# A two-layer attention and expert block: setup, routing, the second layer's keys and values and the first expert tile taken into the first attention

## What is computed

```
x = x + tanh(g_xattn[0]) * L0_xattn(ctx, layernorm(x), mask, ...)   # Perceiver attention
x = x + tanh(g_ffn[0])   * L0_ffn(layernorm(x), weights, indices)   # experts, given routing
x = x + tanh(g_xattn[1]) * L1_xattn(layernorm(x), ctx, ...)         # cross attention to ctx
x = x + tanh(g_ffn[1])   * L1_ffn(layernorm(x), gate_w, w1, w2, w3) # experts, top-2 routing
```

## Time and profile before

| | |
|---|---|
| median of 3 runs | 4273.21 us (4272.74 to 4275.18) |
| the profiled execution | 4271.42 us |
| its span in the profile | 4269.7 us |
| TensorE busy (matmul) | 3954.1 us, 93% |
| VectorE, ScalarE, GpSimd busy | 2978.6, 1977.3, 1009.8 us |
| mean granted TensorE clock | 0.965 of full |

### The profile page before, as it was taken

One profiled execution on the slowest core, in us unless ns is written; L12 is line 12 of the kernel. 1 busy time (PEld: TensorE's weight loads), 2 busy tenths in 40 slices (PEclk: granted clock), 3 DMA queues, 4 the chain that ended last, 5 costly groups with the idle time before them and its releaser, 6 DMA issues. The chain is left out here.

```text
span 4269.7 us, 68747 instructions
## 1 busy us (share of the span) xinstructions
PE 3954.1 (93%) x23968; PEld 3192.9 (75%) x23968; DVE 2978.6 (70%) x4625; ACT 1977.3 (46%) x2806; POOL 1009.8 (24%) x1012
## 2 busy tenths in 40 slices
PE   5999999998499999999988999958999999999998
PEld 3566655564399999999974555548999999999998
DVE  3766666765476676676634888657887887778885
ACT  3655555554154444444423544504444444444443
POOL 3221121210011011011013566403222222222221
PEclk9999999999699999999998999969999999999999
DMA  2000000000366666666640122116666666666664
GB/s 94 20 32 30 30 30 19 23 17 20 110 215 205 208 207 206 207 207 206 206 146 18 60 81 78 40 46 213 215 208 211 214 209 214 210 212 211 209 213 124
DMA packets 376608, 578.80 MB, mean 136 GB/s; under 512 B 25960, under 2 KB 186792, under 8 KB 376488
## 3 DMA queue, kind: packets, MB, share of 16 engines
q1 hardware_dynamic: 344024, 503.50, 35.4%
q0 software_dynamic: 26208, 61.68, 5.8%
q10 hardware_dynamic: 6256, 12.06, 0.8%
HBM read 518.31 MB, written 58.86 MB: 135 GB/s over the span
## 5 line engine op out<-in xcount | busy, mean ns | idle before, releaser
L1115 DVE TENSOR_TENSOR e_WL<-e_raw,e_WH 128x2048 fp32r<-128x2048 f32 x418 | 957.3, 2290 | 475.5 <-ACT e_WH L1064 473.0
L1064 ACT ACTIVATE e_WH<-e_raw 128x2048 fp32r<-128x2048 f32 x418 | 798.8, 1911 | 796.5 <-PE bank L1042 581.4
L1026 PE MATMUL bank<-e_xh,e_WH 128*128 128x256 f32 x3968 | 1127.0, 284 | 38.7 <-ACT e_hf L1080 19.1
L1026 PE MATMUL bank<-e_xl,e_WH 128*128 128x256 f32 x3968 | 1126.5, 284 | 0.0
L1026 PE MATMUL bank<-e_xh,e_WL 128*128 128x256 f32 x3968 | 1126.4, 284 | 0.0
L1026 PEld LDWEIGHTS bank<-e_xh,e_WH 128*128 128x128 f32 x3968 | 765.6, 193 | 42.2 <-issue 28.6
L1026 PEld LDWEIGHTS bank<-e_xl,e_WH 128*128 128x128 f32 x3968 | 765.5, 193 | 2.3
L1026 PEld LDWEIGHTS bank<-e_xh,e_WL 128*128 128x128 f32 x3968 | 765.3, 193 | 0.0
L1042 PE MATMUL bank<-e_WH,e_hh 128*128 128x512 f32 x1360 | 534.9, 393 | 0.0
L1042 PE MATMUL bank<-e_WH,e_hl 128*128 128x512 f32 x1360 | 529.6, 389 | 0.0
L1042 PE MATMUL bank<-e_WL,e_hh 128*128 128x512 f32 x1360 | 528.9, 389 | 0.0
(11 more groups left out here) (216 smaller groups left out, 6097.6 us busy)
## 6 DMA issues: line engine op xcount, KB each, us to landing
e_raw<-in_w SPq DMA_DIRECT2D x262, 1024.0 KB, 5.3
e_raw<-in_w SPq DMA_DIRECT2D x312, 512.0 KB, 4.4
y<-e_Yo ACTq DMA_DIRECT2D x23, 512.0 KB, 2.9
a_X<-in_x SPq DMA_DIRECT2D x32, 256.0 KB, 2.6
a_R<-in_x SPq DMA_DIRECT2D x32, 256.0 KB, 3.8
x<-a_R SPq DMA_DIRECT2D x32, 256.0 KB, 2.0
a_X<-x SPq DMA_DIRECT2D x32, 256.0 KB, 3.4
x<-a_X SPq DMA_DIRECT2D x32, 256.0 KB, 2.0
```

What stands on the lines that cost most here:

```text
L1026: mm = nc.tensor.matmul(up[n % RING][:, q * ROWS:q * ROWS + ROWS], w, x[:, c, :], start=(c == 0 and i == 0), stop=(c == DC - 1 and i == 2))
L1064: act.activation(WH[:, p, :], raw[:, s, :], ACT.Copy).then_inc(high_ready.sem, 1)
L1115: dve.tensor_tensor(WL[:, p, :], raw[:, p % 2, :], WH[:, p, :].bitcast(F32), ALU.subtract)\
```

## The change

Setup, routing and the second attention's keys and values are no longer parts of their own. They stand in `attention0`, on each engine's list ahead of body -1 and in its steps. What moves:

- The gate, routing and small parameter loads (14) are issued from ScalarE's queue at its start, ahead of the tanh. SyncE's queue loads `ctxT` and `wk1` first, then x, `wv1` and the weights (one load more, `wlkvT` in two), and the zeros of the spare rows last.
- TensorE does the counting matmuls, then ten groups of keys and values ahead of body -1; six more and the 32 inversion matmuls follow in its steps. ScalarE adds the key bias and stores each group to new DRAM tensors `kT1` and `V1` (a ring of two). The value bias is added in `attention1`, on the transposed output.
- The weight split of `attention0` is in three parts, between the groups of keys and values.
- In body 7 GpSimd gathers tile 0's x, SyncE loads its first pieces, ScalarE and VectorE split three (steps 8, 10, 13), and VectorE norms x (10, 14); in body 8 TensorE transposes it. Two more pieces are loaded behind the last x1 stores.
- SyncE no longer waits for the x1 stores at the block's end; ScalarE does in `experts`. The attention's semaphores are given back after the first experts.
- In `experts`, for both layers, tile 0 is written out. The pieces not yet split and those of tile 1 are split one behind each slot. In layer 1, which has nothing split ahead, three pieces are split before the first slot.
- `attention1` loads `kT1` and `V1`, 2 MB each, behind its weights.

The core of the diff:

```diff
+AHEAD = 3
+KV_FIRST = 10
+KV_AT = {1: (10,), 3: (11,), 5: (12,), 7: (13,), 9: (14,), 11: (15,)}
+HIGH_AT = {4: 0, 6: 1, 8: 2}
+ROUTE_AT = {s: (3 * s, 3 * s + 1, 3 * s + 2) for s in range(10)} | {10: (30, 31)}
+SPLIT_AT = {8: 0, 10: 1, 13: 2}
 # attention0, sync
+                for dst, src in ((ctxT, "ctxT"), (wk1, "wk1")):
+                    sp.dma_start(dst, ins[src].rearrange("(c p) n -> p c n", p=P)).then_inc(kv_in, 16)
                 for t in range(QT + 1):
                     load_x(0, t)
+                sp.dma_start(wv1, ins["wv1"].rearrange("(c p) n -> p c n", p=P)).then_inc(v_in, 16)
...
-                for t in range(QT):
-                    sp.wait_ge(r_stored[t], 16 * B)
+                    if b == B - 1:
+                        wait_filled(sp, B - 2, ("tk", QT))
+                        sp.wait_ge(r_done, 1)
+                        e = x0.expert_of(sp, 0)
+                        for p in range(AHEAD):
+                            x0.load_piece(sp, e, 0, p)
+                for p in range(AHEAD, AHEAD + 2):
+                    x0.load_piece(sp, e, 0, p)
 # gpsimd
+                        if (b, s) == (B - 1, 2):
...
+                            x0.fetch(pool, 0)
+                        if (b, s) == (B - 1, 12):
+                            x0.root(pool, 0)
 # tensor
-                pe.wait_ge(folded, 3)
+                pe.wait_ge(masks, 2)
+                pe.wait_ge(r_hot, 1)
+                nc.tensor.matmul(pre_b, k.tri[:, :], flat, start=True, stop=True)
+                nc.tensor.matmul(tot_b, k.ones[:, :], flat, start=True, stop=True).then_inc(r_counted, 1)
+                for j in range(KV_FIRST):
+                    keys_values(j)
                 for b in bodies:
                     for s in range(STEPS):
                         if softmax(b):
                             scores(b, s)
+                        elif b < 0:
+                            for j in KV_AT.get(s, ()):
+                                keys_values(j)
+                            for a in ROUTE_AT.get(s, ()):
+                                invert(a)
+                        if (b, s) == (B, 1):
+                            pe.wait_ge(exp_done, 2 * 16 * B)
+                            x0.turn(pe, 0, x0_turn)
 # scalar
+                def keep_keys(j):
+                    act.wait_ge(kv_done, j + 1)
+                    if j >= 2:
+                        act.wait_ge(kv_stored[j % 2], 16 * (j // 2))
...
+                act.wait_ge(gate_in, 32)
+                act.activation(k.gate[:, :], graw[:, :], ACT.Tanh).then_inc(tanhed, 1)
+                act.wait_ge(tanhed, 1)
+                act.wait_ge(small_in, 16 * 10)
+                for j in range(KV_FIRST):
+                    keep_keys(j)
+                    if j in HIGH_AT:
+                        i = HIGH_AT[j]
+                        act.wait_ge(raw_w_in[i], 16)
+                        act.activation(wh[:, :, i * D:i * D + D], raw[i], ACT.Copy).then_inc(w_high, 1)
+                        if b == B - 1 and s in SPLIT_AT:
+                            x0.split_high(act, 0, SPLIT_AT[s], True)
 # vector
+                assignments()
+                slots()
                 for t in range(QT + 1):
                     stats(0, t)
...
+                low(0)
+                low(1)
+                low(2)
+                        if b == B - 1 and s in SPLIT_AT:
+                            x0.split_low(dve, 0, SPLIT_AT[s])
+                        if (b, s) == (B - 1, 10):
+                            x0.norm(dve, 0)
+                        if (b, s) == (B - 1, 14):
+                            x0.scale(dve, 0)
 # experts
         def tiles(eng, body):
-            with eng.Fori(0, nt - 1) as j:
+            body(0, True, True)
+            with eng.Fori(1, nt - 1) as j:
                 body(j, True)
             body(nt - 1, False)
+        first_pieces = [(0, p) for p in range(lead, PIECES)] + [(1, p) for p in range(PIECES)]
-                for p in range(PIECES):
-                    split(0, p, True)
+                for p in range(split, lead):
+                    x.split_high(act, 0, p, True)
                 act.wait_ge(warmed, 1)
+                for r in stored:
+                    act.wait_ge(r, 16 * B)
+                        if first:
+                            jj, p = first_pieces[n]
+                            x.split_high(act, jj, p, jj == 0)
 # attention1, sync
-                for dst, src in ((wk, "wk1"), (ctxT, "ctxT"), (wv, "wv1")):
-                    sp.dma_start(dst, ins[src].rearrange("(c p) n -> p c n", p=P)).then_inc(kv_in, 16)
+                sp.dma_start(kT[:, :, :], k.kT1).then_inc(kv_in, 16)
+                sp.dma_start(V[:, :, :], k.V1).then_inc(kv_in, 16)
```

More of the change, by code:

```diff
@@ L487, in empty @@
                     else:
-                        bb = b - 1 if t == 3 else b
+                        if (b, t) == (0, 0):
+                            for i in range(2):
+                                act.wait_ge(kv_stored[i], 16 * N_KV // 2)
                         i = act.activation(OT[:, t, :], m, ACT.Copy)
@@ new lines, in split_high @@
+    def split_high(self, act, j, p, first=False):
+        if not first:
+            if p < self.UP:
+                act.wait_ge(self.up_done.sem, self.up_done.have(j, 2 * p + 1) - self.SLOTS)
+            else:
+                act.wait_ge(self.down_done.sem, self.down_done.have(j, p - self.UP) - self.DOWN)
+        s, a = p % 2, p // 2 + 1
+        here = min(a, self.UP // 2) * self.raw_step + max(a - self.UP // 2, 0) * 16
+        act.wait_ge(self.raw_in[s], j * self.raw_round + here)
+        act.activation(self.WH(p), self.raw[s], ACT.Copy).then_inc(self.high_ready.sem, 1)
@@ L994, in _, with body @@
                 else:
[L995 to L997 removed]
+                    with pool.Fori(1, nt) as j:
+                        x.fetch(pool, j)
+                        x.root(pool, j)
             @block.tensor
             def _(pe):
[L1001 to L1013 removed]
+                if not done_x:
+                    pe.sem_inc(x_read.sem, x_read.credit)
+                    x.turn(pe, 0, trb)
+                def body(j, more, first=False):
                     pe.wait_ge(xT_ready.sem, xT_ready.have(j, MT - 1))
@@ L1108, in _ @@
             def _(dve):
[L1109 removed]
+                for c in (h_ready, hf_ready):
                     dve.sem_inc(c.sem, c.credit)
                 dve.memset(warm[:, :], 0.0).then_inc(warmed, 1)
[L1113 to L1116 removed]
@@ L1148, in _ @@
-                norm(0)
-                scale(0)
-                columns(0)
-                for p in range(PIECES):
-                    split(0, p)
-                def body(j, more):
-                    if gated:
-                        dve.wait_ge(wnext_ready, j + 1)
+                if not done_x:
+                    for c in (xT_ready, w_ready):
+                        dve.sem_inc(c.sem, c.credit)
+                    x.norm(dve, 0)
+                    x.scale(dve, 0)
+                    x.columns(dve, 0, trb)
@@ L1157, in body @@
+                for p in range(split, lead):
+                    x.split_low(dve, 0, p)
+                def body(j, more, first=False):
+                    if gated:
+                        dve.wait_ge(x.wnext_ready, j + 1)
                         dve.wait_ge(y_ready.sem, y_ready.back(j, MT - 1, MT))
```

696 lines of the change are left out of this document (400 added, 296 removed).

## The result

The changed kernel takes 4237.7 us (median of 4 runs, 4233.8 to 4240.0), the kernel before beside it 4274.2 (4272.7 to 4276.8): 0.991 of it, 95% interval 0.990 to 0.992. Forecast was 4204.9 in a range of 4170 to 4240: the time lies 2.3 us inside the upper end. The direction is as forecast; of the 68 us expected, 37 came. The profiled execution, one of the four and the fastest, took 4233.8 with a span of 4231.9, against 4269.7 before.

What follows compares the result with a forecast made beforehand. TensorE is full in the steady expert loops, so only the stretches where it stands still can gain; 23 + 9.5 - 67 + 6.2 - 34 - 6 = -68.3 us from 4273.2 gives 4204.9 us, range 4170 to 4240.

Steps and rivals of the forecast that it cites:

- Rival A: Start: early groups paced by store landings or late small loads, +38 us instead of +23; 4225 us; chance 0.13.
- Rival B: First experts, tile 0: TensorE's stops keep its late part at the lower clock, 33 us more; 4234 us; chance 0.08.
- E: Rival: gather or pieces not ready by the end of the first attention, -40 us instead of -67; 4232 us; chance 0.04.
- The start: Start to the first attention's first scores: at 121.7 us instead of 98.3, +23 us (+12 to +38).
- The small loads: Start: on ScalarE's queue they land soon (2.9 us seen); at 15.7 us the groups would begin some 12 us later.
- The last softmax body: First attention, body 7: the splits and norm put there lengthen it by 9.5 us (+2 to +17).
- To the second tile: First attention's last result to tile 1 of the first experts: tile 1 begins at 66 us, not 133.2, -67.
- Semaphores: After the first experts: giving back the attention's semaphores there costs +6.2 us (5 to 8).
- Second attention: First load to first scores: 49 us instead of 83, because batch 1's x lands at 28; -34 us.
- Second experts, first tiles: Written-out tile 0 removes TensorE's 11.0 us stop; outputs copied at 2932.7 instead of 2939.4, -6 us (-9 to +2).
- The second loop: Steady tiles of the second experts: unchanged, 0 us.
- Rival D: Expert loops fall behind if a piece takes over 6.1 us a round, not 4.85; at 6.5, 4344 us; chance 0.03.

Runs made afterwards that it cites:

- invert_last: The changed kernel with the inversion products of each step of the opening body put behind that step's own products on TensorE: 4223.2 us.
- all3: The changed kernel with six edits (inversions, next x, batch 1's x, old second-expert beginning, padding among them), without TensorE's empty fills ending both attentions: 4190.2 us, ratio 0.980.
- x_before_kv: The changed kernel with batch 1's x loaded ahead of the stored keys and values in the second attention: 4232.3 us.
- e1_old_start: The changed kernel with the old beginning of the second experts, all six pieces of tile 0 split first: 4238.9 us.
- e1_addr: The changed kernel with an unused 1632-byte buffer restoring the 2048-byte-multiple distance between h and weight pieces in the second experts: 4227.9 us.
- before_shift: The kernel before with an unused 32-byte buffer ahead of the h buffers in both expert stages: 4296.5 us, against 4268.2 without it.

## Why the prediction was half right

The forecast was 32.8 us too low, and that the time still lies in its range is luck: 2.3 us lie between it and the upper end, and the second measurement, 4240.4, would lie outside. The rivals A, B and E name times near the measured one (4225, 4234, 4232), but none of them is what happened. A and B are taken up below. E did not come: the third piece was split at 1079.1 and x of tile 0 scaled at 1084.8, before the last result at 1118.5.

**The start, +35.4 for +23.** The tanh was well placed: counting products at 11.8 us for 13. The sum of TensorE's work, 2.3 + 42.6 + 9.6 + 49.2 = 103.7, meets the measured 104.0 partly by luck: at the clock of 0.98 in `invert_last` the same work took 99.5, so the terms were some 4 us too large and the slower clock filled them. The step that failed is "of the old 13 us of waits I leave 5, those of the late steps, where nothing is put in": 17.9 us remained, 10.2 of them for one-hot pairs. I costed the inversions as TensorE's work and had VectorE "done near 40", but did not follow VectorE's order through the steps, where each set of pairs stands behind the last step's round trip. `invert_last` showed it. That it gives 121.4 us, nearly the forecast's 121.7, is luck again: TensorE still stands for 9.8 us there, not 5, and its smaller work and a tanh 0.9 us earlier make up for it. Rival A (stores or small loads pace ScalarE), +38, would have given nearly the measured start for a wrong reason: TensorE's waits for the copies came to 3.2 us. The stores of keys took 5.0 and 5.6 us to land (medians of the two buffers) and those of values 2.4, against the "some 4 us" that the step asked for.

The small loads were a question of the queues. On ScalarE's own queue the last of them, the mask, issued at 8.7, held ScalarE's first copy for 6.7 us, until 17.6, and TensorE for only 0.6. So it took up to 8.9 us to land, between the 2.9 and the 15.7 us of the earlier trace rows, and the groups did not begin 12 us later. So far the trace agrees with the taking of turns that the Trainium skill, "DMA: Bandwidth & Descriptors", Queues, rings and completion order, describes; it does not prove it.

```profile
8.72 0.61 ACTq L531 DMA_DIRECT2D a_masked_out<-in_mask  x1
...
17.60 0.66 ACT L539 ACTIVATE a_OT<-bank,a_bk 128x480 f32<-128x480 f32 x1 [6.73 <-DMA a_masked_out<-in_mask]
```

**The last softmax body, +3.9 for +9.5.** Right in kind, too large in size: I had two low halves exposed with 2.8 us each. The waits are there: in the last 119 us before the last result TensorE waited 11.6 us for ScalarE's exponentials in the kernel before, in the last 123 of the changed one 18.5, the longest 6.0 us instead of 1.8. The whole stretch grew by only 3.9; where the rest was made up is open.

**To the second tile, -59.6 for -67.** "TensorE starts tile 0 at 2" failed: it was 9.2. The trace of before had the same time in the same place (next operation 9.3 us behind the last result), and I took it for waiting on stores and giving back. The empty fills on TensorE stand there in its place: `all3` has 2.6. From TensorE's start the step held: x of tile 1 was scaled 35.4 us on (forecast 38.3), with one long wait, 8.8 us, ahead of the turn. Rival B, the cold tile, did not come: the clock was 0.92 and 0.87 in its two parts, a short dip, so the oscillation of which the Trainium skill, "TensorE: Matmul & The Clock Gate", HAM oscillation, warns is not what this trace shows.

```profile
1127.70:1150.00 22.30, 21.90 (x168) 21.70 (x168) 12.08 (x10) 12.13 (x10) 4.02 (x2) 0.92 0.60 206
1150.00:1188.20 38.20, 28.64 (x128) 24.14 (x129) 28.33 (x28) 16.00 (x13) 5.53 (x5) 0.87 0.63 210
```

**Semaphores, +1.3 for +6.2.** The "like place" of the earlier trace rows was no like place: most of its 6.3 us were 18 empty fills on TensorE (without them the gap fell by 5.5), and giving back was 0.8. The two errors are one. What I booked as a price of 6 us there and left out as one of 7 at the start of tile 0 is the same thing, steps that only wait for and count semaphores. In the sum they nearly cancel, 4.9 us too much against 7.2 too little, which is luck.

**Second attention, -34.6 for -34.** Right with its reason (`x_before_kv`), S+48.4 for S+49; most other traces had S+51.0 to S+51.6, so as a rule the gain is some 2 us smaller. What follows it in that stage, forecast as 0, is longer in all twelve traces, as said.

**Second experts, first tiles, +4.1 for -6.** Two steps failed. First, I took the copy of the outputs on ScalarE for the end of the tile. TensorE had begun tile 1 before it, at 2935.2, and ScalarE was late with the copy because a split that waited for its piece stood in front of it, so what stood to gain was less. Second, I followed the last h but not the columns of the next x, which stand on VectorE behind slot 7's low half, whose piece lands late: TensorE waited 4.1 us for them, then ran 11.6 us at a clock of 0.76. `e1_old_start` shows the written-out tile to be the loss, 3 to 6 us.

**The second loop, +10.9 for 0.** Rival D said that the loops could fall behind, by pieces coming late; there was no wait at all. The loss came through buffers that moved by 416 bytes, which no step of mine looked at: I compared instructions, not addresses. `e1_addr` and `before_shift` settle that from both sides.

## What to carry to other kernels

When work is put into a stage written out by hand, each engine's list must be followed step by step: what one engine must make for another goes behind a round trip if it stands behind that step's own products. An idle gap read as the price of one thing should be compared with a second place with and without that thing; here two gaps had their cause in something else. And after a change of buffers, one steady tile should be laid beside its old trace, product by product: 0.3 us in a tile is invisible on the page and 11 us in the sum.

## What was unexpected in the hardware

- TensorE's products with 128 stationary and 512 moving float32r columns follow each other in 0.227 us (10.91 for 48) when the buffers of the two operands lie a multiple of 2048 bytes of a partition apart, and in 0.233 (11.20) with 32 or 416 bytes more. Moving both together did not matter. Products with 256 moving columns, 0.120 us each, took the same at 0 and at 416 bytes (48 products, 5.76 us).
- On TensorE an empty fill, a wait and two counts of semaphores, took 0.33 us here (28 in 9.15 us). Behind the last product nothing hid it: the next stage began only 1.4 us behind TensorE's mark, though the other three engines' marks stood 8 us and more earlier.
- The second attention of one program took 503.7 us in one execution and 512.8 in another, with TensorE's granted clock at 0.92 and 0.80 in 50 us near its end. Why the clock falls in one execution and not in another stays open.
